# A post-norm transformer block on one core: the state's scan in halves ahead of the small tables, and one more sequence's one-hot rows on GpSimd

## What is computed

```python
delta = sigmoid(x @ W_t.T + b_t) * 0.99 + 0.01            # 4 sequences x 1024 tokens, D = 256
Bu = x @ W_b.T + b_b                                      # 16 states
_, h = associative_scan(combine, (exp(A * delta), Bu))    # h[t] = a[t] * h[t-1] + Bu[t]
y = (h @ W_c.T + b_c + x * D) @ W_o.T + b_o
x = layernorm(x + y)
top_vals, top_idx = top_k(softmax(x @ Wg), 2)             # 8 experts, 2 for each token
out = sum over the chosen experts of score * (relu(x @ W1[e] + b1[e]) @ W2[e] + b2[e])
```

## Time and profile before

| | us |
|---|---|
| median of 3 runs | 1659.32 |
| lowest, highest | 1657.69, 1660.31 |
| profiled execution, its own time | 1654.58 |
| its span, first to last instruction | 1652.8 |
| TensorE busy | 1549.2 (94%) |
| VectorE busy | 1294.7 (78%) |
| ScalarE busy | 923.4 (56%) |
| GpSimd busy | 288.9 (17%) |
| mean granted TensorE clock, share of full | 0.977 |

### The profile page before, as it was taken

How to read it: one execution, slowest core, us unless ns; L and a number is a source line. 1 busy time by engine, 2 the same in 40 slices (tenths; PEclk the granted TensorE clock), 3 DMA queues, 4 the chain that set the end, 5 groups by cost and what they waited for, 6 DMA issues and landing times.

```text
span 1652.8 us, 29366 instructions
## 1 busy us (share of the span) xinstructions
PE 1549.2 (94%) x11202; PEld 991.8 (60%) x11202; DVE 1294.7 (78%) x2505; ACT 923.4 (56%) x1406; POOL 288.9 (17%) x383
## 2 busy tenths in 40 slices
PE   5977999999999999899999989999998999999986
PEld 2747899999853333785433378643336864333674
DVE  3585466553359998897999979799998979999596
ACT  1222344444137888444788844468885355888632
POOL 0063233221401120301111021111110210000030
PEclk8988999999989999999999999999999999999998
DMA  4125877776333220002421000232200022220000
GB/s 142 51 77 167 254 246 253 247 252 212 92 52 81 53 44 9 1 1 64 88 55 43 13 1 1 64 77 53 55 15 1 1 49 55 40 40 2 1 1 26
DMA packets 80310, 123.13 MB, mean 74 GB/s; under 512 B 13657, under 2 KB 55898, under 8 KB 80170
## 3 DMA queue, kind: packets, MB, share of 16 engines
q1 hardware_dynamic: 70794, 93.46, 21.5%
q0 software_dynamic: 9376, 27.80, 5.9%
HBM read 76.84 MB, written 18.61 MB: 58 GB/s over the span
## 4 chain that ended last, share of the span: by engine, by line
PE 73%; DVE 16%; ACT 5%; issue 3%; DMA 2%; POOL 1%; SPq 1%; DVEq 0%; POOLq 0%; ACTq 0%
PE PS L1116 15%; PE PS L1069 13%; PE PS L992 7%; PE PS L1102 7%; PE PS L980 6%; DVE MX L1656 6%; PE PS L1224 4%; PE PS L1234 4%; PE PS L1039 3%; PE PS L1053 2%; PE PS L925 2%; PE PS L1261 1%; PE PS L969 1%; DMA Pb<-W 1%; PE PS L1186 1%
## 5 line engine op out<-in xcount | busy, mean ns | idle before, releaser
L1656 DVE TENSOR_REDUCE MX<-PS 128x1 f32<-128x512 f32 x1024 | 635.4, 683 | 28.9 <-PE PS L1069 25.5
L774 ACT ACTIVATE Pb<-PS 128x1024 f32<-128x1024 f32 x512 | 519.4, 1026 | 124.7 <-PE PS L1102 124.7
L1069 PE MATMUL PS<-Ks,Qs 48*128 48x512 f32 x1024 | 386.6, 453 | 1.5 <-DVE MX L1656 0.9
L1102 PE MATMUL PS<-Qs,Ks 50*128 50x512 f32 x1024 | 360.0, 451 | 0.0
L1116 PE MATMUL PS<-Pb,V 128*32 128x256 f32 x4096 | 320.5, 390 | 0.5
L1069 PEld LDWEIGHTS PS<-Ks,Qs 48*128 48x128 f32 x1024 | 159.9, 184 | 203.7 <-DVE MX L1656 143.1
L1116 PEld LDWEIGHTS PS<-Pb,V 128*32 128x32 f32 x4096 | 83.9, 108 | 164.2 <-ACT Pb L774 112.8
L1102 PEld LDWEIGHTS PS<-Qs,Ks 50*128 50x128 f32 x1024 | 143.8, 185 | 24.0 <-ACT Pb L774 19.8
L992 PE MATMUL PS<-Pb,OT 128*128 128x256 f32 x624 | 141.0, 379 | 0.0
L980 PE MATMUL PS<-Ks,Qs 128*128 128x256 f32 x936 | 127.4, 294 | 7.2 <-DVE Ks L1528 7.2
L980 PEld LDWEIGHTS PS<-Ks,Qs 128*128 128x128 f32 x936 | 119.7, 197 | 9.7 <-DVE Ks L1528 8.6
(11 more groups left out here) (296 smaller groups left out, 2167.3 us busy)
## 6 DMA issues: line engine op xcount, KB each, us to landing
Pb<-W SPq DMA_DIRECT2D x78, 512.0 KB, 4.3
y_slot<-V SPq DMA_DIRECT2D x39, 256.0 KB, 4.0
Qs<-Qh SPq DMA_DIRECT2D x128, 64.0 KB, 2.3
Ks<-Kh SPq DMA_DIRECT2D x120, 64.0 KB, 2.3
V<-b SPq DMA_DIRECT2D x39, 128.0 KB, 3.7
XT<-x_mid POOLq DMA_DIRECT2D x4, 1024.0 KB, 6.5
out<-Pb POOLq DMA_DIRECT2D x4, 1024.0 KB, 6.7
OT<-xT SPq DMA_DIRECT2D x2, 1024.0 KB, 6.4
```

Source lines behind the costliest of these rows:

```text
L774: F["ex"].inc(act.activation(weights_of(n), PS[:, 2 * (n % 2):2 * (n % 2) + 2, :], ACT.Exp, scale=0.25))
L1069: F["slp"].inc(pe.matmul(PS[:, slot_bank(i), :], Qs[rows, p % NB, t * P:(t + 1) * P], Ks[rows, p % NB, kh * HALF:(kh + 1) * HALF], start=T ...
L1102: ins = pe.matmul(PS[:, 2 * (n % 2) + a, :], Ks[rows, p % NB, kt * P:(kt + 1) * P], Qs[rows, p % NB, qh * HALF:(qh + 1) * HALF], start=Tru ...
L1656: F["sld"].inc(dve.tensor_reduce(MX[:, p % 2, a, t, kh:kh + 1], PS[:, slot_bank(i), :], AX.X, ALU.max))
```

## The change

Three things. The sigmoid, its exponential and the recurrence are done in two halves of 512 tokens, the second recurrence starting from the first's last column, and VectorE's small tables stand behind both; TensorE waits for the first half before `state_out(0)` and for the second before `state_out(1)`. GpSimd makes `lowhot` of sequence 2 as well, behind a wait for `place(1)`, with a signal after each sequence, and TensorE waits for these one at a time. Ten constants stand where 14 stood.

```diff
--- before.py
+++ after.py
@@ -489,13 +489,14 @@
         def _(pool):
             pool.memset(ones[:, :], 1.0).then_inc(s_one, 1)
 
-            pool.wait_ge(C["lw"].sem, 1)
-            for b in range(2):
+            for b in range(3):
+                if b != 1:
+                    C["lw"].wait(pool, 1 + b // 2)
                 for k in range(2):
                     for t in range(TT):
                         ins = pool.tensor_scalar(lowhot[b][:, k * TT + t, :], lane[:, :], low[:, b, k, t:t + 1],
                                                  token[:, b * TT + t:b * TT + t + 1], ALU.is_equal, ALU.mult)
-            C["lh"].inc(ins)
+                C["lh"].inc(ins)
             for q in range(2):
                 C[f"mid{q}"].wait(pool, 16 * B // 2)
             pool.wait_ge(C["ix"].sem, 2)
@@ -633,7 +634,8 @@
             C["hm"].inc(act.activation(Hm, PS[:, 7, 0:D], ACT.Copy))
             act.wait_ge(s_proT, 2)
             act.wait_ge(s_pro, 2)
-            act.activation(aa.rearrange('p (h n) -> p h n', h=NH), PS[:, 0:2, :], ACT.Exp, scale=-1.0, bias=cols[:, 6:7]).then_inc(s_proA, 1)
+            for h in range(NH):
+                act.activation(aa[:, h * HALF:(h + 1) * HALF], PS[:, h, :], ACT.Exp, scale=-1.0, bias=cols[:, 6:7]).then_inc(s_proA, 1)
             act.activation(bu.rearrange('p (h n) -> p h n', h=NH), PS[:, 2:4, :], ACT.Identity, bias=cols[:, 2:3]).then_inc(s_proA, 1)
             act.wait_ge(C["ht"].sem, 1)
             C["hte"].inc(act.activation(XT[:, 1, 0:D], PS[:, 6, 0:D], ACT.Copy))
@@ -643,8 +645,9 @@
             for b in range(B):
                 ins = act.activation(Hz[32 * b:32 * b + 32, b, D:DW], PS[32 * b:32 * b + 32, 5, 4 * E:5 * E], ACT.Copy)
             C["hw"].inc(ins)
-            act.wait_ge(s_scan, 1)
-            act.activation(aa[:, :], aa[:, :], ACT.Exp, scale=cols[:, 0:1]).then_inc(s_proA, 1)
+            for h in range(NH):
+                act.wait_ge(s_scan, 1 + h)
+                act.activation(aa[:, h * HALF:(h + 1) * HALF], aa[:, h * HALF:(h + 1) * HALF], ACT.Exp, scale=cols[:, 0:1]).then_inc(s_proA, 1)
 
             def normalise(h):
                 b, q = h // 2, h // 2 % 2
@@ -910,12 +913,14 @@
                 ins = pe.matmul(PS[:, 5, 4 * E:5 * E], HmT[:, o, :], wgc[:, o, :], start=(o == 0), stop=(o == DC - 1))
             C["hw"].inc(ins)
             pe.wait_ge(C["hw"].sem, 2)
-            pe.wait_ge(s_scan, 2)
+            pe.wait_ge(s_scan, 3)
 
             def state_out(h):
                 b = h // 2
                 if h >= 2:
                     pe.wait_ge(C["lc"].sem, h - 1)
+                if h == 1:
+                    pe.wait_ge(s_scan, 4)
                 for q in range(4):
                     if h >= 2:
                         pe.wait_ge(C["xn"].sem, 4 * (h - 2) + q + 1)
@@ -951,9 +956,10 @@
                     pe.wait_ge(C["rd"].sem, 1)
                 state_out(h)
             ranks(1)
-            warm(14, 2)
-            pe.wait_ge(C["lh"].sem, 1)
+            warm(10, 2)
             for b in range(B):
+                if b < 3:
+                    C["lh"].wait(pe, b + 1)
                 pe.wait_ge(C["ah"].sem, b + 1)
                 for n in range(2 * TT):
                     ins = pe.matmul(PS[:, 3, 0:COLS], lowhot[b][:, n, :], highhot[b][:, n, :],
@@ -1302,11 +1308,20 @@
             for c in range(DC):
                 ins = dve.scalar_tensor_tensor(wgc[:, c, :], PS[:, 5, 0:E], -1.0 / D, wg_sb[:, c, :], ALU.mult, ALU.add)
             C["wgc"].inc(ins)
-            dve.wait_ge(s_proA, 1)
-            pro(dve.tensor_scalar(aa[:, :], aa[:, :], 1.0, None, ALU.add))
-            pro(dve.reciprocal(aa[:, :], aa[:, :]))
-            pro(dve.tensor_scalar(aa[:, :], aa[:, :], 0.99, 0.01, ALU.mult, ALU.add))
-            dve.sem_inc(s_scan, 1)
+            for h in range(NH):
+                ah = aa[:, h * HALF:(h + 1) * HALF]
+                dve.wait_ge(s_proA, 1 + h)
+                pro(dve.tensor_scalar(ah, ah, 1.0, None, ALU.add))
+                pro(dve.reciprocal(ah, ah))
+                pro(dve.tensor_scalar(ah, ah, 0.99, 0.01, ALU.mult, ALU.add))
+                dve.sem_inc(s_scan, 1)
+
+            for h in range(NH):
+                at = slice(h * HALF, (h + 1) * HALF)
+                dve.wait_ge(s_proA, 4 + h)
+                pro(dve.tensor_tensor_scan(hh_sb[:, at], aa[:, at], bu[:, at],
+                                           hh_sb[:, HALF - 1:HALF] if h else cols[:, 3:4], ALU.mult, ALU.add))
+                dve.sem_inc(s_scan, 1)
 
             pro(dve.tensor_tensor_scan(below[:, :], ones_sq[:, :], ident[:, :], 0.0, ALU.mult, ALU.add))
             pro(dve.tensor_tensor(below[:, :], below[:, :], ident[:, :], ALU.subtract))
@@ -1319,9 +1334,6 @@
             pro(dve.memset(keep[:, :], 1.0))
             pro(dve.memset(keep[:, :].rearrange("p (e t) -> p e t", t=T2)[:, :, 0], 0.0))
             pro(dve.memset(count[:, :], 0.0))
-            dve.wait_ge(s_proA, 3)
-            pro(dve.tensor_tensor_scan(hh_sb, aa[:, :], bu[:, :], cols[:, 3:4], ALU.mult, ALU.add))
-            dve.sem_inc(s_scan, 1)
 
             def norm(h):
 
@@ -1382,9 +1394,8 @@
                 pro(dve.tensor_copy(lowi[:, bb, :, :], posr[:, bb, :, :]))
                 pro(dve.tensor_scalar(lowi[:, bb, :, :], lowi[:, bb, :, :], P - 1, None, ALU.bitwise_and))
                 pro(dve.tensor_copy(low[:, bb, :, :], lowi[:, bb, :, :]))
-                if g == 0:
-                    dve.sem_inc(C["lw"].sem, 1)
-                    C["lw"].seen += 1
+                dve.sem_inc(C["lw"].sem, 1)
+                C["lw"].seen += 1
 
             def weights(g):
 
@@ -1454,9 +1465,9 @@
             pro(dve.tensor_copy(tab[:, :], tv[0:1, :]))
             dve.sem_inc(C["tab"].sem, 1)
             high_hot(1)
-            for b in range(2, B):
-                low_hot(b)
-                high_hot(b)
+            high_hot(2)
+            low_hot(3)
+            high_hot(3)
             weights(1)
 
             pro(dve.tensor_tensor(hot[:, :, 1:E - 1], past[:, :, 0:E - 2], past[:, :, 1:E - 1], ALU.subtract))
```

## The result

| | before | after |
|---|---|---|
| median of 10 runs, us | 1658.49 (1657.33 to 1660.31) | 1664.67 (1662.34 to 1666.31) |
| profiled execution, own time / span, us | 1654.6 / 1652.8 | 1665.5 / 1663.7 |

The changed kernel is slower: the ratio is 1.0034, 95% interval 1.0026 to 1.0043. I had predicted 1654.3 in 1650.5 to 1658.7; the median lies 6.0 us above that range. The two profiled executions lie 10.9 us apart and the medians 6.2, because the profiled execution of before ran 3.9 us under its median and that of after 0.8 over its own. Three executions among the experiments took 1.4 to 2.1 times as long as the rest (one of e4, one of e9, one of before beside e4, e5, e7 and e8); they are left out of every ratio.

The account below looks back on a forecast made before the run. TensorE was taken to be bound by its wait for VectorE's recurrence, then by its own constants ahead of the one-hot products. Gains of 3.9 and 1.1 made 5.0 us: 1659.3 - 5.0 = 1654.3, range 1650.5 to 1658.7.

Parts of the forecast that it names:

- The scan: Sigmoid, exponential and recurrence in halves: TensorE starts at 39.3 instead of 43.23, 3.9 us earlier; second recurrence hidden.
- The constants: Ahead of the one-hot products: four constants fewer are eight records, 3.4 us, all gained if the engines were undisturbed.
- The toll on GpSimd: Third one-hot group beside VectorE: 2.7 us for three `highhot` and 0.4 for shorter instructions; ready at 124.1, not 121.0.
- it loses 1.4 less some 0.5: 0.9 for each: GpSimd's third group: average loss for each of VectorE's three `highhot` of 1.4 us, 2.7 us in all.
- The bound of 6 us: GpSimd's third group: upper bound of its toll, both long tolls in full and a little for all 16 instructions.
- The toll on VectorE: One-hot rows: at most 0.16 us for each of GpSimd's 16, 2.6 in all, about 0.9 before the first `highhot`.
- The last rival: One-hot rows: the lock holds for GpSimd's whole 0.79 us, so the kernel is slower, 1664.4 us; chance 0.06.
- TensorE behind the wait: One-hot products: TensorE waits for GpSimd to 124.2, then 127.8 and 131.4 against 132.4 before; 1.0 to 1.1 us gained.
- The new wait cools TensorE: One-hot products: a 2.0 us gap lowers the clock for three microseconds, costing 1.6 us, giving 1655.9; chance 0.22.
- Both arguments against it: Against the cooling at the one-hot products: the gap is a little shorter than 2.07 us, and a long busy stretch precedes it.
- What lies behind the products: `idx`, gathers and expert stage: released by the last one-hot product, so time saved before it is saved in the end.

Follow-up runs that it names:

- e4: Kernel before with only the scan in halves, and ten constants instead of 14: 1661.60 us, ratio 1.0010 against before.
- e9: e8 with 100 identity products instead of 130 ahead of the attention: 1647.69 us, ratio 0.9915 against before, from four runs.
- e5: Changed kernel with five more constants between the products of the second and the third sequence: 1658.60 us, ratio 0.9999 against before.
- e7: Changed kernel with eight of VectorE's `low_hot(3)` ahead of the third `highhot` and eight behind: 1668.67 us in one run.
- e8: Changed kernel with sequence 2's one-hot rows shared, eight by GpSimd and eight by VectorE, and 11 constants: 1654.81 us, ratio 0.9970 against before.
- e1: Kernel before with only the scan in halves, one-hot rows and 14 constants as before: 1655.71 us, ratio 0.9985 against before.
- e6: Changed kernel with VectorE held behind `place(1)` until GpSimd's third group is done: 1679.94 us in one run.
- e3: Changed kernel with 14 constants instead of ten: 1662.15 us, ratio 1.0019 against before.
- e10: Kernel before with 100 identity products instead of 130 ahead of the attention: 1654.09 us, ratio 0.9998 against before.
- e11: Changed kernel with 100 identity products instead of 130: 1660.78 us, ratio 1.0042 against before.

## Why the prediction was wrong

My sum kept before's clock readings less the 3.9 us of the scan. Set on the trace of after, it asked for the first one-hot product at 111.2, for the third sequence at 120.3 and for the end at 127.5. Measured: 111.6, 122.9 and 136.9. So 9.4 us are missing: 0.4 at the start, 2.2 by GpSimd, and 6.8 by the clock. The medians lie 11.2 us from the forecast difference (6.2 slower for 5.0 faster); the 1.8 beyond the 9.4 are not found up to the last of these products, and no run shows their cause.

- **The scan** (3.9): 3.53 in the trace. The halves came as reckoned (3.35 for 3.36, 1.28 for 1.25); 0.3 us is ScalarE's input, which was later in that execution. The second recurrence and the tables were hidden, and the statistics caught up within the first norm. Right; e1 shows it alone.
- **The constants** (3.4): their row is 3.2 us shorter (11.05 for 14.29). Right as an arrangement, wrong as a gain: I booked them as time to be won, and named nothing that they cover. They kept TensorE at work until its inputs were there. e4 shows what leaving them out costs by itself, some 4 us (3.0 in the traces: 131.3 for 128.3), and e8, which left out only three and had all inputs in time, keeps its gain.
- **The toll on GpSimd** (3.1): 5.4 by e6's 12.39, and 5.1 over the 12.7 that I had reckoned. The step "it loses 1.4 less some 0.5: 0.9 for each" was too kind. Each long instruction of VectorE cost 1.1 in the mean, the shorter ones together 1.0 and not 0.4, and four of the long ones were in reach instead of three, for, once late, GpSimd was still at work when the last `highhot` came. The bound of 6 us that I had given held.
- **The toll on VectorE** (up to 2.6): some 0.5 (4.50 for 4.19 at `low_hot`, 0.82 for 0.69 at L1454). The last rival, by which each would have waited 0.79, is refuted: the first `highhot` was ready at 111.2. The Trainium skill, "SBUF — State Buffer", section "SBUF: two separate sides", has an exclusive lock for the whole instruction; the trace agrees in one direction, GpSimd waits for VectorE's long instruction to end, and not in the other: three of the four `highhot` of after start while an instruction of GpSimd's is under way (the first at 109.74, GpSimd's ends at 110.19) and take 1.46 to 1.49, where they took 1.46 in before.
- **TensorE behind the wait**: this is the step that failed. I wrote "waits for GpSimd to 124.2; then 127.8", which is 3.6 for a sequence, the full clock, right behind a new gap of 2 us. Measured 7.1 and 7.0, from 122.9 to 136.9: 14.0 us for 7.2, 6.8 lost. I had the mechanism as a rival ("The new wait cools TensorE") at 0.22, and priced it at 1.6 after the 3 us window of the earlier trace rows. The row was of another load: the products of 264 columns there were back at the upper level after some 3 us, those of 78 columns stayed down as long as they ran (14 us in after, 27.5 in e6). Which property of the load decides, no run tells apart. The window of before's trace behind that of the earlier trace rows shows it back:

```profile
91.00:93.00 2.00, 2.00 (x11) 1.00 0.73 241
```

  With 6.8 in place of 1.6 that rival gives 1654.3 + 6.8 = 1661.1, and 1663.7 with GpSimd's further 2.2 and the 0.4 at the start, near the 1664.7 measured. Both arguments against it were idle. My gap was to be a little shorter than 2.07, but 1.47 (e3) and 1.79 (e4) were followed by a fall too, while 0.63 (e1) wasn't; and TensorE came to it from 18 us of work (100.7 to 118.9). The last rival had the same price too low by its own rows: half the clock adds 3.57 to a sequence, so its last two at the lower level cost 7.1 more, not 3.6, and it should have read 1667.9.
- **What lies behind the products** I took as carried over unchanged. Roughly so: the medians are 6.2 and, with e10 and e11, 6.7 us apart, where the products' ends are 4.5 and 4.2 apart. A single pair of traces says less, since the wait for `w_gate` at the third tile (5.88 us before L1491 in after) and the gaps among the identities shift by some us between executions of one kernel. The distance between the second and the third tile was 6.7 to 9.3 us over the runs, in no relation to the edits; that is left open.

## What to carry to other kernels

Filler work on TensorE ahead of a stretch of small matmuls isn't idle time to be won: before it is cut, each input behind it has to be shown in time with something to spare, since here a gap of 1.5 us was enough, in the execution that was profiled, to double the time of what followed. A fall of the clock is to be priced over the whole stretch behind it, by a row of matmuls of the same shape, not by the nearest fall in the trace. Work given to GpSimd beside VectorE is to be priced by the long two-input instructions that VectorE has under way meanwhile, each at most of its length (0.9 to 1.2 us for 1.46 here), and halved rather than moved whole when it comes out close.

## What the hardware showed that I had not expected

- Products of 128x78, back to back, never brought the granted clock up from 0.50: 13.87 us busy of 14 in after, 27.57 of 28 in e6. The same products hold the upper level when no gap stands ahead of them (15.00 us busy of 15 in e8).
- The clock can fall with a delay: in e3 the gap of 1.47 us ended at 122.41; the window 121 to 124 still has 1.00, and 125 to 134 has 0.50.
- GpSimd's instruction of 0.79 us waited through two of VectorE's back to back (2.92 us); it didn't slip in between.
- In 11 of the 14 traces TensorE pauses about 1 us at a time within the identity products, 7.3 to 9.6 us in all, with no engine named as releaser; the first trace of before, e10 and e11 have no pause. What makes it pause was not found.
